# Mixture of 8 experts: scaling by the gain behind the up products, and the down product in three rounded parts

## The reference

```python
scores = jax.nn.softmax(logits, axis=-1)
top_vals, idx = jax.lax.top_k(scores, K)
weights = jnp.take_along_axis(scores, idx, axis=1)
xs = xt[:, None, :] * weights[:, :, None]
for e in range(E):
    mask = (idx == e)
    h = silu(einsum('tkd,hd->tkh', xs, w1[e]) + b1[e])
    x2 = einsum('tkh,dh->tkd', h, w2[e]) + b2[e]
    x3 = einsum('tkd,hd->tkh', xs, w3[e]) + b3[e]
    y = y + sum(x2 * x3 * mask[:, :, None], axis=1)
z = (silu(xt @ sw1.T) * (xt @ sw2.T)) @ sw3.T
return y + z
```

## Time and profile before

| | us |
|---|---|
| median of 3 runs | 2521.76 (2521.12 to 2527.99) |
| profiled execution | 2514.52 |
| its span, first to last instruction | 2512.4 |
| PE busy | 2363.1 (94%) |
| DVE, ACT, POOL busy | 1721.3, 1469.8, 1108.8 |
| mean granted TensorE clock | 0.972 |

### The profile page before, as it was taken

How to read it: one execution, slowest core, us unless ns; L and a number is a source line. 1 busy time by engine, 2 the same in 40 slices (tenths; PEclk the granted TensorE clock), 3 DMA queues, 4 the chain that set the end, 5 groups by cost and what they waited for, 6 DMA issues and landing times. The chain is left out here.

```text
span 2512.4 us, 93734 instructions
## 1 busy us (share of the span) xinstructions
PE 2363.1 (94%) x38650; PEld 1990.5 (79%) x38650; DVE 1721.3 (69%) x3254; ACT 1469.8 (59%) x4030; POOL 1108.8 (44%) x1092
## 2 busy tenths in 40 slices
PE   7999999999889999998689998999999889899999
PEld 6899999999877888886476666777777678888888
DVE  4777777777686776776878866777777656555453
ACT  4656665666576666665565656777777644422222
POOL 2444444444340000002657775666666533355555
PEclk9999999999999999998879998999999989799999
DMA  6554444444261111110055312100011100177564
GB/s 209 217 187 156 151 161 165 151 151 153 75 260 60 50 42 42 42 42 2 8 110 97 73 35 63 31 25 25 25 30 27 37 26 0 32 123 135 107 124 79
DMA packets 69013, 221.64 MB, mean 88 GB/s; under 512 B 7232, under 2 KB 21060, under 8 KB 60044
## 3 DMA queue, kind: packets, MB, share of 16 engines
q1 hardware_dynamic: 68878, 219.77, 30.4%
HBM read 198.11 MB, written 21.64 MB: 87 GB/s over the span
## 5 line engine op out<-in xcount | busy, mean ns | idle before, releaser
L579 POOL TENSOR_TENSOR l_pn<-l_probs,l_rden 128x1024 f32<-128x1024 f32 x128 | 242.5, 1895 | 402.6 <-DVE l_rden L415 402.6
L512 ACT ACTIVATE l_probs<-ps,l_nmax 128x257 f32<-128x257 f32 x512 | 236.3, 475 | 241.7 <-DVE l_nmax L409 226.7
L981 POOL TENSOR_TENSOR l_probs<-l_probs,l_rden 128x1024 f32<-128x1024 f32 x128 | 242.5, 1895 | 170.1 <-DVE l_rden L832 170.1
L917 ACT ACTIVATE l_probs<-ps,l_nmax 128x257 f32<-128x257 f32 x512 | 236.4, 475 | 59.6 <-DVE l_nmax L826 59.6
L409 DVE TENSOR_REDUCE l_nmax<-ps 128x2 f32<-128x514 f32 x256 | 165.0, 685 | 122.2 <-PE ps L291 122.2
L2868 POOL TENSOR_TENSOR m_hh<-m_hh,m_cb 128x512 f32<-128x512 f32 (+1 forms) x136 | 179.7, 1323 | 142.0 <-DVE m_hh L2820 128.6
L291 PE MATMUL ps<-l_ctxQ,l_q 32*128 32x257 f32 x3072 | 202.7, 392 | 9.4 <-ACT l_q L519 9.2
L2724 ACT ACTIVATE m_sg<-ps 128x512 f32<-128x512 f32 (+1 forms) x136 | 81.5, 599 | 220.1 <-PE ps L111 219.3
L2820 DVE TENSOR_TENSOR m_hh<-ps,m_sg 128x512 f32<-128x512 f32 (+1 forms) x136 | 93.9, 691 | 167.5 <-PE ps L111 151.6
L826 DVE TENSOR_REDUCE l_nmax<-ps 128x2 f32<-128x514 f32 x256 | 165.4, 688 | 61.0 <-PE ps L718 57.2
L837 DVE COPY l_pT<-ps 128x512 f32<-128x512 f32 x256 | 164.8, 686 | 52.3 <-PE ps L727 48.1
(11 more groups left out here) (376 smaller groups left out, 6289.1 us busy)
## 6 DMA issues: line engine op xcount, KB each, us to landing
l_ctxQ<-in_ctx_q SPq DMA_DIRECT2D x32, 1542.0 KB, 6.6
m_cb<-combined SPq DMA_DIRECT2D x64, 512.0 KB, 10.9
l_ctxK<-in_ctx_k SPq DMA_DIRECT2D x16, 1536.0 KB, 6.5
l_early<-in_ctx_k SPq DMA_DIRECT2D x16, 1536.0 KB, 6.7
enc_dash<-kept SPq DMA_DIRECT2D x32, 512.0 KB, 3.4
l_ctxT<-in_ctx_t SPq DMA_DIRECT2D x32, 385.5 KB, 3.4
m_cb<-combined SPq DMA_DIRECT2D x16, 768.0 KB, 16.2
kept<-enc_va SPq DMA_DIRECT2D x10, 512.0 KB, 3.0
```

Source lines behind the costliest of these rows:

```text
L512: nc.scalar.activation(probs[:, par % 2, hg, :], ps[:, S_B + hg, 0:NK], ACT.Exp, bias=nmax[:, par, hg:hg + 1], accum_out=den[:, par, hg:hg ...
L579: nc.gpsimd.tensor_tensor(pn[:, b % 2, :, :], probs[:, b % 2, :, 0:NK - 1], rden[:, b, :, None].to_broadcast([P, HG, NK - 1]), ALU.mult).t ...
L917: nc.scalar.activation(probs[:, b, hg, :], ps[:, S_B + hg, 0:NK], ACT.Exp, bias=nmax[:, b, hg:hg + 1], accum_out=den[:, b, hg:hg + 1]).the ...
L981: nc.gpsimd.tensor_tensor(pr, pr, rden[:, b, :, None].to_broadcast([P, HG, K_W]), ALU.mult).then_inc(norm_ok, 1)
```

## The change

- Products up read the unweighed input `xg` for every expert. `cb` multiplies both products of a unit at once afterwards, on DVE (`scale`, 128x1024 from the two PSUM banks to `scaled` in SBUF). POOL's `weigh`, ACT's `high` and DVE's `low` are gone.
- PE may write the banks of unit v-2 again once `scale` (for a shared unit, `shared`) has read them; before it was ACT's `g3`.
- ACT takes silu twice from `scaled`, once in f32 (`hh`) and once rounded to fp32r (`hs`, high part), and then the identity with bias. POOL takes the rest (`unit_low`). The product down is three products with w2, which is split in preparation as well (ACT, POOL).
- Ranks: DVE makes the two comparisons (`compared`), POOL the rest in five instructions that add halves (`ranked`), DVE the last two (`kept`).
- The turn of the gains of group 0 stands one step later on PE and ACT, and the split of the input of group 0 is earlier.

The core of the diff:

```diff
@@ preparation @@
+                nc.scalar.copy(w2_wide[:, 0, :], w2[:, :]).then_inc(wh_ok, 1)
...
+            ranked(0)
             for n, src in enumerate((w1, w3)):
                 weights_low(n, src)
...
+            pool.wait_ge(wh_ok, 4)
+            nc.gpsimd.tensor_tensor(w2_wide[:, 1, :], w2[:, :], w2_wide[:, 0, :].bitcast(F32),
+                                    ALU.subtract).then_inc(wl_ok, 1)
-            for n in range(4):
-                weigh(n)
@@ PE: up and down @@
             def up(v):
-                g, b = v // UNITS, v % 2
+                g, b = v // UNITS, UP + 2 * (v % 2)
                 if v > 1:
-                    pe.wait_ge(act_ok, v - 1)
                     if is_shared(v - 2):
                         pe.wait_ge(sh_ok, shared_no(v - 2) + 1)
                     else:
-                        pe.wait_ge(g3_ok, expert_no(v - 2) + 1)
+                        pe.wait_ge(sc_ok, expert_no(v - 2) + 1)
...
-                    pe.wait_ge(act_ok, v + 1)
+                    pe.wait_ge(hl_ok, n + 1)
                     if n > 1:
                         pe.wait_ge(y_ok, n - 1)
-                    nc.tensor.matmul(ps[:, X2 + n % 2, :], w2[:, e * D:e * D + D], hh[:, v % 4, :],
-                                     start=True, stop=True).then_inc(dn_mm, 1)
+                    pe.nop(nofuse=True)
+                    product(nc, ps[:, X2 + n % 2, :], [w2_wide[:, m, e * D:e * D + D] for m in range(2)],
+                            [hs[:, v % 4, m, :] for m in range(2)]).then_inc(dn_mm, 1)
@@ ACT @@
-                    nc.scalar.activation(hh[:, v % 4, :], from_up, ACT.Silu, bias=bcols[:, 0, e:e + 1]).then_inc(act_ok, 1)
-                    act.wait_ge(u_mm, v + 1)
+                    act.wait_ge(sc_ok, n + 1)
+                    nc.scalar.activation(hh[:, v % 4, :], scaled[:, n % 3, 0, :], ACT.Silu,
+                                         bias=bcols[:, 0, e:e + 1]).then_inc(act_ok, 1)
+                    nc.scalar.activation(hs[:, v % 4, 0, :], scaled[:, n % 3, 0, :], ACT.Silu,
+                                         bias=bcols[:, 0, e:e + 1]).then_inc(hs_ok, 1)
...
-                    nc.scalar.activation(g3[:, n % 4, :], ps[:, X3 + v % 2, :], ACT.Identity,
+                    nc.scalar.activation(g3[:, n % 4, :], scaled[:, n % 3, 1, :], ACT.Identity,
                                          bias=bcols[:, 2, e:e + 1]).then_inc(g3_ok, 1)
@@ DVE @@
+            def scale(v):
+                n = expert_no(v)
+                g, e = n // E0, n % E0
+                dve.wait_ge(back[g % 2][e // 2], 16 * (g // 2) + 16)
+                dve.wait_ge(u_mm, v + 1)
+                if n > 2:
+                    dve.wait_ge(g3_ok, n - 2)
+                b = UP + 2 * (v % 2)
+                nc.vector.tensor_tensor(scaled[:, n % 3, :, :], ps[:, b:b + 2, :],
+                                        cb[:, g % 2, e, None, :].to_broadcast([P, 2, 512]), ALU.mult).then_inc(sc_ok, 1)
...
+                if i == 2 and g < NG - 2:
+                    compared(g + 2)
+                if i == 7 and g < NG - 2:
+                    kept(g + 2)
@@ POOL @@
+            def unit_low(v):
+                n = expert_no(v)
+                pool.wait_ge(hs_ok, n + 1)
+                nc.gpsimd.tensor_tensor(hs[:, v % 4, 1, :], hh[:, v % 4, :], hs[:, v % 4, 0, :].bitcast(F32),
+                                        ALU.subtract).then_inc(hl_ok, 1)
...
             for v in range(NV + 3):
-                if v + 4 < NV and not is_shared(v + 4) and expert_no(v + 4) > 3:
-                    weigh(expert_no(v + 4))
+                g, i = v // UNITS, v % UNITS
+                if v < NV and not is_shared(v):
+                    unit_low(v)
                 if v > 2 and not is_shared(v - 3):
                     summed(expert_no(v - 3))
+                if v == 0:
+                    ranked(1)
+                if i == 4 and g < NG - 2:
+                    ranked(g + 2)
```

More of the change, by code:

```diff
@@ L2210, in _ @@
                     scored(0, 4, st0, ex0_ok)
-                    rank(0, 0)
-                    rank(0, 1)
+                    compared(0)
                 if g == 3:
-                    for part in (2, 3, 4):
-                        rank(0, part)
-            low(0)
-            low(1)
+                    kept(0)
             centred(4, T, L_B, st)
@@ L2221, in _ @@
                 g, i = v // UNITS, v % UNITS
[L2222 to L2225 removed]
                 if is_shared(v):
                     shared(v)
+                else:
+                    scale(v)
                 if v > 1 and not is_shared(v - 2):
                     weighed(v - 2)
[L2230 to L2231 removed]
                 if i == 8 and g < NG - 1:
```

162 lines of the change are left out of this document (65 added, 97 removed).

## The result

The changed kernel takes 2537.8 us in the median of 14 runs (2522.6 to 2550.5), the kernel before 2528.5 beside it. The ratio is 1.0048, 95% interval 1.0028 to 1.0069: slower by 7 to 17 us, 12 in the middle. The forecast was 2520 and a range of 2505 to 2536, no change likeliest. The kernel before was itself 6.8 us slower beside it than in the three runs that the forecast started from (2521.76), so of the 18 us between 2520 and 2537.8 some 7 are the base and 11 the change.

The account below looks back on a forecast made before the run. PE was taken to bound the kernel, interrupted once a group by the chain POOL weigh, ACT cast, DVE low. The terms summed to -1.6 us, giving 2520 on the median of 2521.76, range 2505 to 2536.

Parts of the forecast that it names:

- preparation: Work before the first up: later POOL lows against no wait for weighing, first up +1.3 us, ends 0 and +4.
- group 0: First ten units, with constants and a wait for POOL's ranks: 29.2 us, a gain of 0.5, ends 28 and 31.
- group 1: Second ten units, no xs to wait for: 28.0 us, a gain of 3, ends 27.4 and 31.0.
- groups 2 to 5: Ranking groups: 23.8 dense plus 3.7 of stops, about 27.4 us each, the same as before.
- group 6: Group without comparisons: stops 0.6, 0.4 and 0.9, so 25.3 us against 25.0.
- group 7 and turn: Last group, low8 at 25.8, four POOL sums to 30.9, then the turn: 31.9 us against 31.6.
- the walk: One ranking group timed from its first up: stops 1.0, 0.5, 0.9, 0.4, 1.0, end at 27.4 us.
- the clock rival: Rival: a group's four stops bring half clock once in each of 8 groups, 13 us slower, 2533; chance 0.10.
- the rival of a front not unloaded: Rival: first up waits longer and group 1 stays at 31, +4 + 3, 2526, still no change; chance 0.04.
- GpSimd's pace: Rival: POOL's instructions take 1.50 us, slowing every low on the path, +8, 2530; decides from about 1.45; chance 0.18.
- Smaller stops: Rival: comparisons take 0.85 us on an idle POOL and silus overlap better, -7 to -15, about 2511; chance 0.28.
- The three rounded parts: Product down: 64 products from 0.86 to 0.70 us, 10.2 us less PE work, 1.3 a group where PE is dense.

Follow-up runs that it names:

- e1: Changed kernel with GpSimd ranking group 1 after low1, and group 0's gains turn and constants one pair of units later; +7 us (2 to 11) over before.
- e10: Changed kernel with the ranks on VectorE again, three instructions a group instead of GpSimd's five; +8 us (2 to 14) over before.
- e2: Changed kernel with VectorE's two comparisons one unit earlier, behind scale1, in groups 1 to 5; +4 us (-1 to 8) over before.
- e11: Changed kernel with plain f32 down, both scales of a pair first except units 8 and 9, input's parts and count moved; ratio 0.9944 to before.
- e5: Changed kernel with both scales of a pair first on VectorE and the next input's parts two units earlier; -3 us (-9 to 4) over before.
- e4: Changed kernel with the product down left in plain f32, without second silu, unit_low or parts of w2; -8 us (-13 to -4) over before.
- e7: Changed kernel with comparisons, out, count, the next input's parts and group 0's ranks and constants all moved; +3 us (-3 to 8) over before.
- e3: Changed kernel with both scales of a pair ahead of both weighed on VectorE; +27 us (19 to 36) over before.
- e7b: e7 with both low parts of a pair ahead of the two sums on GpSimd; +37 us (21 to 53) over before.

## Why the prediction was wrong

The sum, term by term, against the means of three profiles before and four after:

| term | predicted | measured |
|---|---|---|
| preparation | +1.3 | 23.6 to 24.7: +1.15 |
| group 0 | -0.5 | 29.0 to 32.2: +3.2 |
| group 1 | -3.0 | 29.7 to 28.2: -1.5 |
| groups 2 to 5 | 4 x 0.0 | 27.3 to 27.9: 4 x 0.6 |
| group 6 | +0.3 | 24.6 to 25.8: +1.15 |
| group 7 and turn | +0.3 | 31.9 to 33.3: +1.35 |
| sum | -1.6 | +7.75 |

Five of the six terms came out on the slow side of the forecast: group 0 by 3.7, group 1 by 1.5, groups 2 to 5 by 2.4, group 6 by 0.85, the tail by 1.05. Together that is 9.5 us; only the preparation came out 0.15 better than forecast.

**Group 0 is the step that failed.** The text set down that it "waits for POOL's ranks between low0 and low1, about 2 us", and still gave it 29.2. The wait was sized well (1.8 to 2.6), its place in the walk was not: it was never set against the 1.6 us of slower slots that the prediction itself priced behind a stop of 2.02 in the clock rival, nor was group 0 walked as a ranking group was. e1 and e10, which take the ranks away from there, give 28.85 and 27.41, so 3.3 to 4.8 of the 32.2 were this one place. The 29.2 would have been right for the order of e1. The clock rival asked of the wrong stops: none of the five in a ranking group, all below 0.8, brought half clock (PEclk 1.00); the one before down1 did in all four profiles.

**Group 1** was right in kind. Its gain was taken from a profile that happened to have a stretch of half clock there; two more profiles of the kernel before have 29.1, so 1.9 of the 3.0 was that execution's. The level, 28.0, was nearly right (28.5, 28.5, 27.9, 27.9).

**Groups 2 to 5: mechanism right, size off by 0.5 to 0.6 each.** All five stops stand where the walk put them (up5, down3, up7, down5, down7), with a comparison of 1.51 and a scale of 1.21 as priced. Their sum was right too: 3.6 by starts, 3.8 in the walk (its sum has 3.7). What the walk has wrong is that everything comes too early:

| | up5 | down3 | up7 | down5 | down7 | end |
|---|---|---|---|---|---|---|
| walk | 12.85 | 15.5 | 18.5 | 21.1 | 26.25 | 27.4 |
| measured, group 4 | 13.14 | 16.02 | 18.77 | 21.65 | 26.78 | 27.9 |

The 0.3 at up5 is there before any stop: down0's slots end at 9.24 and not at 8.95. The first slots of up0 and up2, before which PE isn't idle, are 0.32 and 0.33 long instead of 0.23, and the old downs and constants between them take 0.1 more than walked. Behind up5 come the longer first slots and ACT's activations from SBUF, 0.71 in place of 0.62 to 0.69 (hs3 ends 1.43 behind scale3; the walk has 1.3). None of this adds up from stop to stop, since a stop that waits for another engine takes up what PE lost before it (changed kernel, ACT's and POOL's groups of the stage):

```profile
L2039 ACT ACTIVATE m_hs<-m_scaled,m_bcols 128x512 fp32r<-128x512 f32 x64 | 45.3, 708 | 0.0
...
L2250 POOL TENSOR_TENSOR m_hs<-m_hh,m_hs 128x512 fp32r<-128x512 f32 x64 | 85.3, 1334 | 61.8 <-ACT m_hs L2039 61.4
```

The same holds for **group 6 and the tail**, 0.85 and 1.05 under-sized. Group 6 has stops of 0.42, 0.31 and 0.70 before up7, down5 and down7 and takes 25.8, not 25.3; the other 0.35 is the base, which is 24.6 between first ups and not the 25.0 of the window. The tail has one more before down8 (0.57), and its turn back starts 31.9 behind its first up, not 30.9.

**Preparation** was right to 0.15, and the first up no longer waits for weighing; the rival of a front not unloaded falls. **GpSimd's pace** falls: lows at 1.33 in the mean, below 1.45. **Smaller stops** is what another order gives, not this one: e2, which lets the comparisons run elsewhere, gives 26.27, 1.0 below the 27.3 of before.

**The three rounded parts** would bring what was computed, 1.3 a group (25.3 without stops in e11 against 24.0 for e5 less its stop), but only where PE never waits, and no run with them has such a group. With their silu and low in the changed kernel's order PE has five stops; without them (e4) four of the five are gone. e4 shows the split: the weighing behind the products was worth -8.5 us of stage, the three-part down +16.2.

## What to carry to other kernels

When a step moves to an engine that also feeds the path, walk the first group too, with the once-only work in it: the place where a queue is new and nothing has been buffered is where a wait of 2 us arises, and behind such a wait TensorE may run at half clock. Price each half of a change alone: here the half that takes engines out of the chain pays, and the half that saves slots adds an engine to the chain and lost more than it saved in every order that was run. Once an order has no slack, small moves can cost more than they bring (1.7 us a group in e7, for three of them), so move one thing at a time and read where the next stop comes; e3, e7 and e7b each moved several and couldn't say which one hurt.

## What was not expected of the hardware

A restart of TensorE's row behind a wait costs 0.1 us beyond the idle time (first slot 0.31 to 0.34 against 0.23). In the ranking groups stops of 1.4 to 1.6 (e5, e7) and of 1.65 to 1.9 (the kernel before) were followed by slots at full rate. The stops of 2.0 to 2.9 in e3 and e7b, the 2.02 of the earlier trace rows, and those of 1.8 to 3.4 before down1 of group 0, were followed by records of 0.63, at once or a few matmuls later. But the 2.47 before the changed kernel's last turn back was followed by full slots in three of four profiles, and by slots of 0.21 in place of 0.11 in the fourth, so the length of a stop alone doesn't tell. A DVE instruction of 128x32 that takes 0.18 by itself took 1.33 beside a GpSimd one (e7). And one kernel's executions differ by single steps of 5 to 8 us in stages that nobody changed, so two profiles of each side are needed before a term of 3 us is read from a row.
